# Row maxima turned one step later and in two parts, with all later stages of the attention pipeline two steps later

## The reference

```python
x = x + layernorm(attention(layernorm(x), wq, wk, wv, wo))
x = x + layernorm(ffn(layernorm(x), W_base, b_base, W_gate, A, B))
```

## Time and profile before

| | |
|---|---|
| Median of 3 runs | 269.82 us (265.75 to 270.4) |
| Span of the profiled execution | 265.6 us |
| Lowest run, the one nearest to that span | 265.75 us |
| PE busy | 212.1 us, 80% |
| DVE busy | 170.5 us, 64% |
| ACT busy | 135.9 us, 51% |
| POOL busy | 117.9 us, 44% |
| Share of 16 DMA engines used by SP's queue | 43.8% |

### The profile page before, as it was taken

One profiled execution on the slowest core, in us unless ns is written; L12 is line 12 of the kernel. 1 busy time (PEld: TensorE's weight loads), 2 busy tenths in 40 slices (PEclk: granted clock), 3 DMA queues, 4 the chain that ended last, 5 costly groups with the idle time before them and its releaser, 6 DMA issues.

```text
span 265.6 us, 3792 instructions
## 1 busy us (share of the span) xinstructions
PE 212.1 (80%) x1304; PEld 130.1 (49%) x1304; DVE 170.5 (64%) x414; ACT 135.9 (51%) x238; POOL 117.9 (44%) x93
## 2 busy tenths in 40 slices
PE   0699999977757999699595999695497988997860
PEld 0575734433433444244343444143477967886750
DVE  1983437759738768547473771426457988889674
ACT  2241603312235878558545574643157485777771
POOL 8000506613095867748466334941551452332031
PEclk9999999999979999979998899999979999998985
DMA  6994069898930638666473222223321001110013
GB/s 185 367 379 158 12 233 210 260 299 160 263 114 4 151 115 285 147 161 109 151 147 128 72 88 84 88 76 132 135 68 39 2 0 41 39 42 4 36 41 118
DMA packets 34058, 34.14 MB, mean 129 GB/s; under 512 B 2808, under 2 KB 28536, under 8 KB 34040
## 3 DMA queue, kind: packets, MB, share of 16 engines
q1 hardware_dynamic: 34040, 33.91, 43.8%
HBM read 19.42 MB, written 14.29 MB: 127 GB/s over the span
## 4 chain that ended last, share of the span: by engine, by line
PE 30%; DMA 28%; DVE 22%; ACT 7%; issue 5%; SPq 5%; POOL 2%; POOLq 0%; DVEq 0%; ACTq 0%
DMA region_b<-mrow 10%; DMA den_pk<-o_scr 6%; PE ps L1086 4%; PE ps L1149 4%; DVE stats L743 4%; PE ps L1001 3%; DMA o_scr<-o_sb 3%; PE ps L1060 3%; PE ps L1101 3%; PE ps L977 3%; PE ps L991 3%; DMA region_b<-q_scr 2%; SPq L325 2%; DMA rden_bc<-r_scr 2%; DMA x_sb<-x 2%
## 5 line engine op out<-in xcount | busy, mean ns | idle before, releaser
L917 DVE TENSOR_REDUCE nmax<-ps 128x4 f32<-128x1024 f32 x32 | 39.1, 1223 | 25.3 <-PE ps L1060 25.3
L512 POOL TENSOR_SCALAR_AFFINE_SELECT region_a<-region_a 128x1024 f32<-128x1024 f32 x32 | 35.2, 1106 | 26.7 <-ACT region_a L689 26.6
L1086 PE MATMUL ps<-region_b,kst 99*128 99x512 bf16 x96 | 28.7, 405 | 14.5 <-DMA region_b<-mrow 13.4
L689 ACT ACTIVATE region_a<-ps 128x1024 f32<-128x1024 f32 x32 | 32.7, 1020 | 1.2 <-PE ps L1086 1.2
L686 ACT ACTIVATE region_a<-ps 128x512 f32<-128x512 f32 x32 | 19.1, 598 | 26.0 <-PE ps L1086 25.6
L991 PE MATMUL ps<-region_a,region_c 128*128 128x512 f32 x64 | 29.0, 598 | 0.0
L914 DVE TENSOR_REDUCE nmax<-ps 128x4 f32<-128x512 f32 x32 | 21.8, 683 | 8.4 <-PE ps L1044 8.4
L554 ACT ACTIVATE std<-mv,eps_sb 128x1 f32<-128x1 f32 x32 | 9.3, 293 | 32.3 <-DVE mv L744 32.3
L1101 PE MATMUL ps<-region_a,v_aug 128*32 128x512 f32 x192 | 25.2, 603 | 0.0
L548 ACT ACT_TABLE_LOAD x17 | 21.8, 1283 | 1.1 <-PEq L1246 0.8
L1060 PEld LDWEIGHTS ps<-kst,region_b 96*128 96x128 bf16 x256 | 18.3, 102 | 7.0 <-issue 1.7
(11 more groups left out here) (107 smaller groups left out, 436.6 us busy)
## 6 DMA issues: line engine op xcount, KB each, us to landing
region_b<-q_scr SPq DMA_DIRECT2D x8, 768.0 KB, 8.0
o_scr<-o_sb SPq DMA_DIRECT2D x8, 512.0 KB, 3.1
q_scr<-region_c SPq DMA_DIRECT2D x8, 384.0 KB, 3.6
x_sb<-x SPq DMA_DIRECT2D x8, 256.0 KB, 5.9
q_scr<-region_c SPq DMA_DIRECT2D x8, 256.0 KB, 3.5
attn_t<-o_scr SPq DMA_DIRECT2D x8, 256.0 KB
rden_bc<-r_scr SPq DMA_DIRECT2D x8, 256.0 KB
out<-region_b SPq DMA_DIRECT2D x8, 256.0 KB, 2.0
```

The source lines that it names most:

```text
L512: pool.affine_select(out=blocks, in_=blocks, compare_op=ALU.is_ge, fill=0.0, base=0, pattern=[[0, 2], [0, REP], [1, P]], channel_multiplie ...
L689: nc.scalar.activation(probs[:, u % PRING, 1:3, :], ps[:, 4:6, :], ACT.Exp, scale=float(HEAD_DIM) ** -0.5).then_inc(exp_done, 1)
L917: nc.vector.tensor_reduce(nmax[:, gi % 2, 1, heads], ps[:, 1:3, :].rearrange("p a (r k) -> p r a k", r=REP), AX.XY, ALU.max, negate=True). ...
L1086: last = nc.tensor.matmul(ps[:, 3 + j, :], kst[0:TROWS, slot, k, kt * P:(kt + 1) * P], qst[0:TROWS, slot, k * REP:(k + 1) * REP, qt * P:(q ...
```

## The change

Maxima are split in two bf16 parts (96 + 2 rows in place of 96 + 3), and the residual buffer `nmax_r` goes. MAX_LAG is 6 for 5, ST_LAG 9 for 7, PV_LAG 14 for 12; the loop has 45 steps. `stack_max` issues one transfer for each part, from 16 partitions to one. `invert`, `store_rden` and `spread_rden` come at PV_LAG + 8, + 8 and + 9 for + 6, + 6 and + 7, that is four steps later in all; VectorE inverts the last two groups, not one, after tile step 2. `divide` and the high parts of the quotient move two steps further behind PV_LAG, too. `EARLY` and `EARLY_OUT` follow from the constants: tile steps 0 and 1 at steps 40 and 43, projections at 33 and 40.

```diff
+MAX_PARTS = 2
-TROWS = SROWS + PARTS
+TROWS = SROWS + MAX_PARTS
-ST_LAG = 7
-MAX_LAG = 5
-PV_LAG = 12
+ST_LAG = 9
+MAX_LAG = 6
+PV_LAG = 14
...
             def stack_max(gi):
                 sp.wait_ge(mrow_ready, gi + 1)
-                sp.dma_start(qst[SROWS:TROWS, gi % RING, :, :], mrow[0:PARTS * GROUP_HEADS, gi % 2, :])\
-                    .then_inc(mrow_stacked[gi % 2], 16)
+                for part in range(MAX_PARTS):
+                    sp.dma_start(qst[SROWS + part:SROWS + part + 1, gi % RING, :, :],
+                                 mrow[part * GROUP_HEADS:(part + 1) * GROUP_HEADS, gi % 2, :])\
+                        .then_inc(mrow_stacked[gi % 2], 16)
...
-            for n in range(MAX_LAG, STEPS + 5):
+            for n in range(MAX_LAG, STEPS + 7):
                 for lag, count, what in ((MAX_LAG, GROUPS, stack_max), (PV_LAG + 3, GROUPS, send_out),
-                                         (PV_LAG + 4, GROUPS, fetch_out), (PV_LAG + 6, GROUPS, store_rden),
-                                         (PV_LAG + 7, GROUPS, spread_rden)):
+                                         (PV_LAG + 4, GROUPS, fetch_out), (PV_LAG + 8, GROUPS, store_rden),
+                                         (PV_LAG + 9, GROUPS, spread_rden)):
...
-                b, r = divmod(n - PV_LAG - 12, 8)
+                b, r = divmod(n - PV_LAG - 14, 8)
...
-                if n == PV_LAG + 13:
+                if n == PV_LAG + 15:
                     attn_high_part(0)
...
-                    link(nc.vector.tensor_tensor(left, full, high, ALU.subtract))
-                    link(nc.vector.tensor_copy(mid, left))
-                    nc.vector.tensor_tensor(low, left, mid, ALU.subtract).then_inc(nmax_split, 1)
+                    nc.vector.tensor_tensor(low, full, high, ALU.subtract).then_inc(nmax_split, 1)
...
-                if n == PV_LAG + 21:
+                if n == PV_LAG + 23:
...
-                gi, r = divmod(n - PV_LAG - 6, 4)
-                if r == 0 and 0 <= gi < GROUPS - 1:
+                gi, r = divmod(n - PV_LAG - 8, 4)
+                if r == 0 and 0 <= gi < GROUPS - 2:
                     invert(gi)
...
                 if s == 2:
+                    invert(GROUPS - 2)
                     invert(GROUPS - 1)
...
-                    pe.wait_ge(mrow_stacked[gi % 2], 16 * (gi // 2 + 1))
+                    pe.wait_ge(mrow_stacked[gi % 2], 16 * MAX_PARTS * (gi // 2 + 1))
```

More of the change, by code:

```diff
@@ L129, in build @@
         nmax = sb("nmax", [P, 2, 2, GROUP_HEADS])
-        nmax_r = sb("nmax_r", [P, 2, 2, GROUP_HEADS])
-        nmax_p = sb("nmax_p", [P, 2, PARTS, GROUP_HEADS], BF16)
+        nmax_p = sb("nmax_p", [P, 2, MAX_PARTS, GROUP_HEADS], BF16)
         mrow = sb("mrow", [P, 2, SEQ], BF16)
@@ L694, in _ @@
                     if gi >= 2:
-                        act.wait_ge(mrow_stacked[gi % 2], 16 * (gi // 2))
-                    nc.scalar.copy(mrow[0:PARTS * GROUP_HEADS, gi % 2, :],
-                                   ps[0:PARTS * GROUP_HEADS, 0, 0:P].bitcast(BF16)).then_inc(mrow_ready, 1)
+                        act.wait_ge(mrow_stacked[gi % 2], 16 * MAX_PARTS * (gi // 2))
+                    nc.scalar.copy(mrow[0:MAX_PARTS * GROUP_HEADS, gi % 2, :],
+                                   ps[0:MAX_PARTS * GROUP_HEADS, 0, 0:P].bitcast(BF16)).then_inc(mrow_ready, 1)
                 gi, r = divmod(n - PV_LAG, 4)
@@ L920, in _ @@
                 if k == 0 and 1 <= gi <= GROUPS:
-                    full, left = nmax[:, (gi - 1) % 2, :, :], nmax_r[:, (gi - 1) % 2, :, :]
-                    high, mid, low = (nmax_p[:, :, j, :] for j in range(PARTS))
+                    full = nmax[:, (gi - 1) % 2, :, :]
+                    high, low = (nmax_p[:, :, j, :] for j in range(MAX_PARTS))
                     dve.wait_ge(s12_free, n)
@@ L1068, in turn_max @@
                 for qt in range(2):
-                    last = nc.tensor.transpose(ps[0:PARTS * GROUP_HEADS, 0, qt * 64:(qt + 1) * 64].bitcast(BF16),
+                    last = nc.tensor.transpose(ps[0:MAX_PARTS * GROUP_HEADS, 0, qt * 64:(qt + 1) * 64].bitcast(BF16),
                                                nmax_p[:, qt, :, :].rearrange("p a h -> p (a h)"), ident_bf[:, :])
```

## The result

The changed kernel takes 285.64 us (median of 4 runs, 284.36 to 287.32), the kernel before 268.87 us on the same chip. The ratio is 1.0658 with an interval of 1.0551 to 1.0765: slower by 6.6%, and 0.6 us above the upper end of the predicted range. The profiled execution took 284.36 us, its span is 282.6 us against 265.6 before: 17.0 us more.

A forecast was written before the change was run, and what follows sets the result against it. It took late maxima transfers behind slow four-engine fetches, then the send-to-send chain from 166 us, as the bound. Send delay 7.2, VectorE's restart 0.9 and tail 1.0 gave +9.1: span 265.6 to 274.7, median 278.5 us; range 264 to 285.

The forecast's parts named there:

- The maxima's waits: TensorE's 13.4 us of waits for the row maxima before the transposed scores go, except in the first group.
- alone, this: Later maxima and transposed scores by themselves, without the other terms: span falls from 265.6 to 250.2 us.
- the sum's load waits: q loads 0.3 to 0.7 us late at steps 20 and 24; 4 us wait at step 28, bounds 0 and 6.
- The round: Send to send on SP's queue, with store behind fetch and send behind spread: 12.8 us, bounds 11.4 and 14; before 9.0.
- The hold at step 29: ScalarE waits for GpSimd's divide(0), so TensorE at step 31 starts at 148.9 instead of 142.7 us.
- The sends: Output stores to DRAM: send 4 at 155.9, send 7 at 195.0 us, 7.2 later; VectorE goes on 10.0 after it.
- The tail: After VectorE goes on, divide(3) and the residual addition come later: +1.0 us.
- A: Rival: maxima waits go, rounds keep 9 us, nothing takes their place; 256 us span, 260 median; chance 0.14.
- D: Rival: maxima transfers stay late behind a q load, so waits only move; 270 to 278 us; chance 0.07.
- B: Rival: rounds of 11.4 to 12 us, ScalarE not held at step 29; 266 to 270 us median; chance 0.25.
- C: Rival: load wait at step 28 and rounds both at upper bounds; send 7 near 200, 284 us; chance 0.07.
- the two parts: Maxima split in two parts instead of three: taken as 0; bounds -0.5 to +0.3 us a group.

The follow-up runs named there:

- e5: Kernel before with only the maxima in two parts and two transfers, lags and reciprocals as before: 267.58 us, ratio 1.0017.
- e8: Kernel before with only the three lags changed to 6, 9 and 14, three parts and early reciprocals kept: 277.75 us, ratio 1.0306.
- e1: Changed kernel with the reciprocals back at their old distance (PV_LAG + 6, + 6, + 7), new lags and two parts kept: 271.36 us, ratio 1.0079.
- e4: Kernel before with only the late reciprocals (PV_LAG + 8, + 8, + 9), old lags and three parts kept: 282.19 us, ratio 1.0483.
- e10: Changed kernel with ScalarE's high part of batch 0 three steps later and GpSimd's part two later: 283.32 us, ratio 1.0621.
- e3: Changed kernel with the attn_t fetch and the reciprocals' spread each in four transfers of 16 partitions: 260.44 us, ratio 0.9667 to the kernel before.
- e11: Kernel before with fetch and spread in four transfers each, ST_LAG 8 and PV_LAG 13, three parts: 269.15 us, ratio 1.0125.
- e12: e11 with the maxima in two parts and two transfers: 255.84 us, ratio 0.9533 to the kernel before.
- f2: e11 with GpSimd's eight weight splits moved to steps without the maxima's split: 262.44 us, ratio 0.9808 to the kernel before.

## Why the prediction was right and wrong

**The sum of the parts, by runs and their ratios.** Two parts alone +0.2% (e5, within its uncertainty); lags alone +3.1% (e8); both together +0.8% (e1); late reciprocals alone +4.8% (e4); everything +6.6%, 16.8 us. The direction and its cause were right, the amount was not. In the span, the miss adds up: 282.6 us against 274.7 forecast, 7.9 us, are 5.3 until the last send, -0.3 from there until VectorE goes on, and 2.9 in the tail.

**The maxima's waits** were to go but for the first group. They went, there too. The gain that was to come of it did not: the text had a span of 250.2 us for "alone, this", and e1, which is that with its loads, has a span of 271.3 against 265.6 before. No run has the lags with none of the load waits, so the 250.2 itself stays untested. Of the sum's load waits (0.3 to 0.7 at two places, 4 us at step 28) the changed kernel has 1.05 at 104.55, 0.92 at 116.38 and 5.75 at 133.02: the last under its bound of 6 but over the 4. Its q load took 10.7 us from 122.27 on; the text had 11.4 (10.1 + 1.3), once from 124 on and once with a landing at 133.5, which do not fit each other. The landing, 133.0, fits the second.

**The round was the term that was mis-sized.** The prediction said: "two fetch issues 1.1, then about 4.0 until `attn_t` has landed (3.6 of data, the rest latency, an estimate)". SP's timeline of the kernel after for that round:

```profile
164.72 0.58 SPq L372 DMA_DIRECT2D den_pk<-o_scr  x1
165.34 0.56 SPq L374 DMA_DIRECT2D attn_t<-o_scr  x1
165.94 0.53 SPq L378 DMA_DIRECT2D r_scr<-rden_pk  x1
171.75 0.52 SPq L386 DMA_DIRECT2D rden_bc<-r_scr  x1
172.32 0.46 SPq L360 DMA_DIRECT2D o_scr<-o_sb  x1
```

The send's 7.28 us (predicted 7.0), the fetch issues' 1.2 (1.1) and the spread's issue 0.57 (0.6) are right. From store to spread stand 5.8 us, not 4.0. Rounds are 14.9, 13.6 and 14.4 us where I had 12.8, 13.5 and 12.8, two of them beyond even the upper bound of 14. This step of the prediction failed: the time that a store waits behind the `attn_t` fetch, 4.0 in the text, is 5.8. The 3.6 was a remainder, the lateness of something else behind the fetch, when the profile had a direct price: the spread moves the same 256 KB over the same four engines and takes 6.01 us. With that, less the 0.6 us between the issues of fetch and store, the term would have been 5.4, the round 14.2, and the last send, three such rounds after 155.9, at 198.5 instead of 195.0.

**The hold at step 29** came as predicted: `divide(0)` ends at 145.77 (145.8 predicted), and in the timeline of TensorE after

```profile
148.63 0.58 PE L1041 MATMUL ps<-mask_bf,ident_bf 128*128 128x512 bf16 x1 [5.34 <-ACT mrow L698]
```

where the text had a start that could be at 142.7 and is at 148.9. Send 4 left at 157.42, predicted 155.9. e10 shows that taking this hold away is worth at most some 2 us.

**The sends.** The last left at 200.31, predicted 195.0: of these 5.3 us the three rounds after send 4 make 3.8 and the way to send 4 1.5. VectorE went on 9.7 us after it (predicted 10.0), behind a wait of 10.40 us for the denominators (predicted 8 or more). The stretched round was foreseen only on VectorE: `divide(1)` also held GpSimd, and TensorE 12.06 us behind its masks, which the text does not have.

**The tail** was the second mis-sized term: "+1.0". From the first gating operation to the end it is 72.6 us for 68.8 before. Busy time in windows of 15 us of the kernel after (length, PE, PEld, DVE, ACT, POOL busy, granted clock, DMA share, GB/s):

```profile
216.00:231.00 15.00, 13.85 (x74) 12.64 (x74) 11.11 (x33) 6.29 (x13) 4.89 (x3) 0.88 0.12 36
231.00:246.00 15.00, 12.55 (x61) 10.49 (x59) 13.41 (x48) 10.87 (x21) 4.90 (x3) 0.89 0.05 18
```

At the same distance behind the gating's begin the kernel before has a clock of 1.00 in both:

```profile
203.00:218.00 15.00, 14.28 (x82) 12.52 (x81) 12.72 (x48) 11.34 (x22) 7.34 (x4) 1.00 0.03 7
218.00:233.00 15.00, 13.89 (x81) 12.00 (x81) 13.38 (x52) 9.51 (x22) 5.11 (x4) 1.00 0.09 36
```

Ahead of its first window the kernel after has TensorE waiting 11.08 us, until 214.76. `divide(3)` waits 7.64 us for its spread and runs at 226.73, and beside it

```profile
226.91 2.23 DVE L752 SCALAR_TENSOR_TENSOR nmr<-mv,rstd 128x1 f32<-128x1 f32 x1
229.06 1.56 DVE L757 TENSOR_SCALAR region_b<-x_sb,mv,rstd 128x512 f32<-128x512 f32 x1
```

VectorE holds operations that took 0.16 and 0.54 us ten us earlier. The first ends with GpSimd's (226.73 to 229.12), the second 0.3 us behind GpSimd's next (229.06 to 230.34). TensorE then waits 1.16 us for L757. The tail is long (72.6 to 73.2 us) in just the three kernels whose late stores stand behind the slow fetch (after, e4, e10), and 68.2 to 70.4 in all others. How its 3.85 us divide between the clock, this stall and the late quotient was not separated.

**Rivals.** A (nothing takes the place) was wrong: the store landed late, and even with bare stores, in e1, the time is 271. D had no part: the maxima did not wait. B needed rounds of 11.4 to 12 us, and none came after send 4. C, "both at their upper bounds", with send 7 near 200 and 284, is what came: 200.31, and 285.64 in the median. It was given 0.07, because the bounds for the round came from the estimate and not from the 6.01. That C's total fits so closely is in part luck: it lacks the 2.9 us by which the tail was longer than foreseen, and it adds 4.2 us from span to median, where 3.0 were measured.

**A missing term** was the two parts, held at 0: right at the old lags (e5), some 6 us saved at the new ones (e8 against e1). The cover named for it, "VectorE isn't what waits in mid-loop", was read from a schedule that the same change moved. This term makes the kernel faster, so it is no part of the miss; it hid part of what the deeper lags cost.

## What to carry to other kernels

Look for transfers whose share of the DMA engines shows only a few of them at work, and split these before moving anything: here one edit that moves no work made 254.6 us of 267.9, where the whole change made 285.6 of 268.9. In a serial chain of small transfers each took about the time of the large one issued ahead of it on the queue; price that by a row of the same size and shape, not by the lateness of a bystander. And count small VectorE operations by what GpSimd runs beside them in the new schedule, not in the old.

## What the runs showed of the hardware

One transfer of 256 KB with four outer rows lands in 6.01 us, in four of 16 partitions each in 2.3 us (e3; 3.5 us from first issue to last landing). Issued right behind one of the undivided transfers, a 16 KB store takes 5.4 to 5.9 us for 1.7, and a 512 KB one 7.1 to 7.3 for 2.9 (after).

Small VectorE operations between tiles in SBUF (cast, subtraction, scalar form) stretched from 0.17 to 0.19 us to as much as 3.1 us, in the cases shown each to within 0.3 us of the end of the GpSimd instruction running beside it, while the reductions from PSUM kept their mean of 1.22 us in after, e11, e12 and f2 alike. The Trainium skill, page SBUF — State Buffer, section "Who interferes with whom", states such a rule: a VectorE instruction with two SBUF inputs contends with a GpSimd instruction that reads SBUF, a copy or cast does when it uses two ports, one fully blocks until the other has finished, and a reduction never does. The trace agrees, as far as it shows these forms. How it adds up is seen in e11: with GpSimd's instructions back to back, three small operations in a chain each waited for one of them (0.74, 1.21 and 1.00 us).
